# In two tiles of each sequence, VectorE makes the low part of a unit's second half before the row maxima two units on

## The reference

```
x = x + attention(layernorm(x))
    scores = einsum('bhqd,bhkd->bhqk', q_full, k_full) * scale      # 16 heads, causal
    scores = where(causal, scores, min)
    probs  = softmax(scores, axis=-1)
    attn   = einsum('bhqk,bhkd->bhqd', probs, v)
    out    = attn @ Wo
x = x + moe(layernorm(x))        # router, top 2 of 16 experts, and a shared expert
```

## Time and profile before

| what | value |
|---|---|
| median of three runs | 1637.66 us (1635.73 to 1639.40) |
| profiled execution, first to last instruction (span) | 1659.5 us |
| PE busy / DVE busy / ACT busy / POOL busy | 90% / 78% / 62% / 60% of the span |
| granted TensorE clock, mean | 0.977 |
| one tile 4, exp(0) to exp(15), first sequence | 45.5 us |
| one tile 5, exp(0) to exp(15), first sequence | 48.5 us |

### The profile page before, as it was taken

The page is one execution under the profiler, slowest core; times in us unless marked ns, Lnnn a source line. Parts: engine busy times, 40 slices in busy tenths (PEclk is TensorE's granted clock), DMA queues, the critical chain, the costliest instruction groups (busy, mean ns, idle before and its releaser), DMA issues.

```text
span 1659.5 us, 45247 instructions
## 1 busy us (share of the span) xinstructions
PE 1497.1 (90%) x16430; PEld 1087.0 (66%) x16431; DVE 1289.5 (78%) x3107; ACT 1028.4 (62%) x2344; POOL 990.3 (60%) x1596
## 2 busy tenths in 40 slices
PE   7879999999899999988999999989999998789990
PEld 2556777767667777676677777766777776566660
DVE  3787888888888988877878788878887887455556
ACT  2566766676567666756666666566666665456660
POOL 3357855543687565665877778668777463433440
PEclk9999999999999999999999999999999999899995
DMA  6358733123364231224543223345421212356418
GB/s 186 68 131 175 142 68 59 23 55 63 81 117 81 59 62 25 59 59 85 99 90 68 48 36 62 59 86 105 81 62 39 42 28 62 92 162 200 121 39 308
DMA packets 331032, 144.70 MB, mean 87 GB/s; under 512 B 278498, under 2 KB 321541, under 8 KB 330824
## 3 DMA queue, kind: packets, MB, share of 16 engines
q1 hardware_dynamic: 305744, 105.67, 31.0%
q10 hardware_dynamic: 18168, 19.41, 3.9%
q0 software_dynamic: 6912, 16.83, 3.2%
HBM read 47.04 MB, written 29.53 MB: 46 GB/s over the span
## 4 chain that ended last, share of the span: by engine, by line
PE 60%; DVE 17%; ACT 7%; issue 5%; DMA 4%; SPq 2%; POOL 1%; another core or an unknown queue 0%; ACTq 0%; DVEq 0%; POOLq 0%
PE of_ps L698 25%; PE s_ps L698 21%; PE t_ps L872 13%; DVE pT L1661 5%; DVE smax L1632 2%; ACT pT L1064 2%; DMA qT<-work 2%; DVE smax L1614 1%; ACT work L1064 1%; ACT probs L1193 1%; ACT probs L1198 1%; DVE o_sb L1495 1%; DVE smax L1636 1%; DMA work<-y_exp 1%; PE of_ps L980 1%
## 5 line engine op out<-in xcount | busy, mean ns | idle before, releaser
L1661 DVE TENSOR_TENSOR pT<-t_ps,pT 128x512 f16<-128x512 f32 (+3 forms) x688 | 409.2, 598 | 133.7 <-ACT pT L1064 127.0
L1064 ACT CAST pT<-t_ps 128x512 f16<-128x512 f32 (+3 forms) x688 | 355.0, 516 | 241.1 <-PE t_ps L872 239.9
L698 PE MATMUL s_ps<-kT,qT 128*128 128x512 f16 (+3 forms) x2112 | 474.7, 337 | 4.5 <-DMA qT<-work 4.5
L872 PE MATMUL t_ps<-id,probs 128*128 128x128 f32 x2304 | 381.3, 280 | 34.6 <-DVE pT L1661 17.2
L872 PEld LDWEIGHTS t_ps<-id,probs 128*128 128x128 f32 x2304 | 256.9, 142 | 131.7 <-issue 75.3
L1193 ACT ACTIVATE probs<-s_ps,nmax,fac 128x640 f32<-128x640 f32 (+3 forms) x256 | 269.2, 1052 | 0.1
L698 PEld LDWEIGHTS of_ps<-ckv,pT 128*128 128x128 f16 x6912 | 241.0, 98 | 41.9 <-DVE o_sb L1495 10.1
L698 PE MATMUL of_ps<-ckv,pT 128*128 128x64 f16 x6912 | 257.8, 193 | 7.8 <-DVE o_sb L1495 7.4
L698 PEld LDWEIGHTS s_ps<-kT,qT 128*128 128x128 f16 x2112 | 203.7, 98 | 71.3 <-DMA qT<-work 5.2
L698 PE MATMUL of_ps<-weights,xT 128*128 128x512 f16 (+1 forms) x936 | 197.6, 348 | 19.3 <-ACT work L1064 7.8
L1932 POOL TENSOR_TENSOR os_<-o_sb,os_ 128x512 f16<-128x512 f32 x60 | 70.2, 1170 | 155.2 <-ACT os_ L1064 146.7
(11 more groups left out here) (238 smaller groups left out, 2455.3 us busy)
## 6 DMA issues: line engine op xcount, KB each, us to landing
wgu_sb<-wgu ACTq DMA_DIRECT2D x8, 704.0 KB, 4.9
work<-lists SPq DMA_DIRECT2D x40, 128.5 KB
qT<-lists SPq DMA_DIRECT2D x40, 128.5 KB
x_sb<-x SPq DMA_DIRECT2D x32, 128.0 KB, 2.4
x<-x SPq DMA_DIRECT2D x32, 128.0 KB
dense<-den SPq DMA_DIRECT2D x32, 128.0 KB
weights<-dense ACTq DMA_DIRECT2D x1, 4096.0 KB
qT<-y_exp SPq DMA_DIRECT2D x16, 256.0 KB, 6.6
```

The source lines that it names most:

```text
L698: return pe_.matmul(o, a, b, start=start, stop=stop)
L872: last = pe_.transpose(t_ps[:, h, c * P:(c + 1) * P], probs[:, u % 2, g * L + j * P:g * L + (j + 1) * P], id32[:, :])
L1064: return act.copy(o, i)
L1661: dve.tensor_tensor(pT[:, u % 2, 1, h, 0:w], t_ps[:, h, 0:w], pT[:, u % 2, 0, h, 0:w], ALU.subtract).then_inc(s.lo_p, 1)
```

## The change

`whole_maxima(t, k)` is true in tiles 4 and 5 for slots 0 to 13: there max(k+2) belongs to the same tile, a unit is one head, and the row's maximum is taken in one piece. In those slots DVE now runs lo0(k), lo1(k), max(k+2) in place of lo0(k), max(k+2), lo1(k). That is 14 slots in each of 8 tiles, 112 slots in all. No instruction is added or dropped, and no other queue changes.

```diff
+            def whole_maxima(t, k):
+
+                return k + 2 < units(t) and GROUP[t % TB] == 1 and not SPLIT_MAX[t % TB]
+
@@
                     side(t, k, 0)
                     prob_lo(t, k, 0)
                     side(t, k, 1)
-                    maxima_ahead(t, k)
-                    prob_lo(t, k, 1)
+                    if whole_maxima(t, k):
+                        prob_lo(t, k, 1)
+                        maxima_ahead(t, k)
+                    else:
+                        maxima_ahead(t, k)
+                        prob_lo(t, k, 1)
```

## The result

The changed kernel takes 1650.39 us (median of four runs, 1648.49 to 1651.90), the kernel before 1636.70 (median of four, 1634.38 to 1639.40). The ratio is 1.0079, interval 1.0062 to 1.0096, so the change costs 12.9 us (10.1 to 15.7). The direction and the mechanism were forecast. The time lies above the forecast's own range (to 1648.5) and just inside the range with the rivals (to 1650.5), and the 7.4 us of the sum were too few by 5.5.

A forecast was written before the change was run, and what follows sets the result against it. PE was taken to set the pace, busy about 96% in the stretches of tiles 4 and 5. (1.2 + 0.65) x 4 sequences = 7.4 us, added to the median 1637.7, gave 1645.1 us, range 1638.5 to 1650.5.

The forecast's parts named there:

- the forecast's own range: Whole kernel: 1641.5 to 1648.5 us around the forecast of 1645.1, given a chance of 0.68.
- the 7.4 us of the sum: Tiles 4 and 5 in four sequences: (1.2 + 0.65) x 4 = 7.4 us slower.
- The loop: exp(k+1), hi1(k), lo1(k), max(k+2), `nmax`, exp(k+2): a floor between exps of 2.93 us in tile 5, 2.45 in tile 4.
- bare slots: Slots with no PE side product before the next exp: each costs 0.56 us more in tile 5, 0.17 in tile 4.
- Its last link: The hand-over from `nmax` to exp at the end of the loop, taken as 0.03 us.
- Slot by slot in tile 5: Delays followed through tile 5 of the first sequence: 0.89 to 1.50 us late at its end, 1.2 taken.
- The step that failed: Tile 5: hi0(13) stood 1.70 us until 281.01; if fixed in time, exp(14) is +0.33, if it moves along, +0.94.
- the tile's range: Tile 5 ends 0.89 us late with the hi0(13) stop fixed in time, up to 1.50; 1.2, the middle, taken.
- Tile 4: Tile 4 longer by 0.5 to 0.95 us, 0.65 taken; slots 0 to 7 costed at nothing.
- No change: Rival: PE's idle time elsewhere hides the delay; 0 to +3 us, 1637.7 to 1640.7; chance 0.17.
- Faster: Rival: earlier lo1 ends PE's waits for lo in slots with search or `out_norm`; 4.4 us, 1633.3; chance 0.07.
- VectorE fills up: Rival: standing in tiles 4 and 5 exceeds DVE's idle time; +22.6 us, 1660; in full or part, chance 0.08.

The follow-up runs named there:

- before again: The second trace of the kernel before, with no edit, taken in e0; span 1636.7 us.
- e0: The kernel before once more, no edit, against the kernel before: ratio 0.9989 (0.9973 to 1.0005).
- f1: The changed kernel once more, against the kernel before at 1663.76 us on this chip: ratio 1.0045 (1.0029 to 1.0062), 7.5 us.
- e4: New order in tiles 4 and 5 only in slots 0 to 7 and 10, against the kernel before: ratio 1.0012 (1.0002 to 1.0022), +2.0 us.
- e3: New order in tiles 4 and 5 only in slots 8, 9, 11, 12 and 13, against the kernel before: ratio 1.0099, +16 us.
- e6: The kernel before plus an unused 256-column reduce ahead of the maximum in tiles 4 and 5, against the kernel before: ratio 1.0141, +23.1 us.
- e7: New order in tiles 4 and 5 only in slots 1 and 9, against the kernel before: ratio 0.9979 (0.9959 to 0.9999).
- e9: The changed kernel with the searches of tiles 4 and 5 moved to other slots, against the kernel before: ratio 1.0033 (1.0013 to 1.0052).
- f2: New order in tiles 4 and 5 only in slots 1 and 9, once more, against the kernel before: ratio 0.9981 (0.9969 to 0.9992).

## Why the prediction came out as it did

**The loop: right.** It closes, in the bare slots that follow one another, with lo1 released by hi1, and the exps wait for `nmax`. Forecast floors 2.93 and 2.45 us, measured 3.01 and 2.53.

**Its last link: mis-sized.** I took 0.03 us for the hand-over from `nmax` to exp, from a hand-over inside VectorE. From VectorE to ScalarE it is 0.10 (284.44 to 284.54). With lo1's 0.35 for 0.33 this makes the loop 0.08 us longer, in at most five bare slots of eight tiles: at most 3.2 us of the missing 5.5, less what product slots hide.

**Slot by slot in tile 5.** Against before again, the first sequence's tile changes by +0.40, +0.22 and -0.55 in slots 0 to 2 (sum +0.07, forecast 0); +0.49 and -0.38 for slots 6 and 7; +0.64, +0.20, -0.55 for slots 8 to 10 (sum +0.29, forecast +0.38); and +0.65, +0.56, +0.41 for slots 11 to 13, 1.62 in all. The forecast had 0.56, then between -0.61 and 0, then 0.56.

**The step that failed** is the one on hi0(13), "If that is fixed in time it swallows part of the delay". The 1.70 us stop isn't there where the runs take 1637 us; it stands in traces of chips where they take 1663. The record doesn't name the first trace's chip, but its span is of that kind. On the chips of the timed runs exp(14) follows exp(13) after 2.45 us, there is nothing to swallow, and slot 12 pays 0.56. Both ends of the tile's range have this wrong: the lower lets the stop take up 0.61, and the upper, where the stop moves along, still charges slot 12 nothing. With e0's distances (2.37, 2.45, 2.60) the same steps give 0.38 + 0.56 + 0.48 + 0.33 = 1.75, and with the longer loop 1.99. The first sequence has 2.08, the others up to 2.44. The clue was in the text: a span 22 us over the median. I noted that the same two tiles stand in both, and should have asked what in the trace can't be in the runs. On the slower chip of f1 the measured cost is 7.5 us, the forecast 7.4. That is luck: the tiles of its trace are 10.5 us longer, not 7.4, and the hand-over and tile 4 were too small there too.

**Tile 4: too small.** Forecast 0.65, measured 1.97, 1.41, 1.66 and 1.16. The three last bare slots give 0.27 + 0.25 + 0.27 = 0.79, not 0.34 to 0.51, since the loop is 2.53 and not 2.45 and no stop takes anything up. The rest is in slots 0 to 10, where I costed slots 0 to 7 at nothing: in the first sequence slots 0 to 2 give +0.63.

**Rivals.** No change: wrong. Faster: wrong for the change as a whole, but right as a mechanism in slots 1 and 9. VectorE fills up: a small part, at most the 2.0 us of e4 in time (0.3 to 3.6). The Trainium skill's advice (Perfetto Trace Analysis, Optimization Strategy) to find the gaps of the engine in question and what each waits for held here: TensorE's gaps grew by exp, lo and `out_norm`, while no busy share moved by over one point. The Trainium skill's 125 ns for VectorE on PSUM (Perfetto Trace Analysis, Optimizing Scalar/DVE Operations), with 0.27 us for 256 columns (0.60 less 0.33), would make lo1 of tile 5 an estimated 0.40 us; it took 0.33 to 0.35 us to the next start, so the row was the better guide.

## What to carry to other kernels

In in-order queues, an instruction put ahead of another brings its wait along. Before swapping two, ask what releases the first one, and whether that releaser itself waits, an engine or two further on, for the second; if so, a loop closes, and its length is a floor under the period wherever no longer work lies beside it. Follow the old order round in the same way: here it had a loop of 2.52 us, and the swap put one of 3.01 in its place. Do the swap only in the places where the engine gets there later than the operand: two slots of sixteen gained 0.2% on chips where all fourteen cost 0.45%. And when the trace's span and the runs' median differ by more than the effect that is forecast, don't count a stop of unknown cause as cover.

## What the runs showed of the hardware

The same kernel takes 1637 to 1640 us on two chips (e0 to e3, e4 to e6) and 1663 to 1664 on two others (e7 to e9, f1 and f2). Each chip was used at one time only, so that it is the chip itself isn't shown. The granted clocks (medians 0.980 and 0.977) differ by 0.3%, the times by 1.5%. The slower ones have single distances between two exps that are longer by 0.2 to 1.8 us, at much the same places of the program each time; at the one in the earlier trace rows ScalarE waits on until 281.01 for a transpose that the row of TensorE shows as over at 279.83. The faster ones don't show them there. The change costs 0.79% (0.62 to 0.96) on the one kind and 0.45% (0.29 to 0.62) on the other, so a ratio measured on one chip needn't be the ratio on another. A semaphore's hand-over was 0.03 us inside VectorE and 0.02 to 0.03 from ScalarE to VectorE, but 0.10 from VectorE's `nmax` to ScalarE's exp.
